# Moving the next head's projection to the second step of a block, and the out-projection to the third

## The chip, the cores and the metric

The kernel runs on one core of one Trainium2 chip. The metric is the time of one execution on the device in microseconds (us). Before the change the median of two runs is 1168.97 us (1168.78 to 1169.16).

## The reference, cut to what matters

The input `x` has 2 batches of 1024 tokens with 128 features. It is layer-normalised to `xn`; the output is `x` plus a differential attention of `xn` plus a mixture-of-experts feed-forward of `xn`. The attention takes nearly all of the time:

```python
Q = einsum('bse,hec->bhsc', X, Wq) + bq      # 16 heads, 2*64 columns
K = einsum('bse,hec->bhsc', X, Wk) + bk
V = einsum('bse,hed->bhsd', X, Wv) + bv
A1 = einsum('bhqd,bhkd->bhqk', Q1, K1) * s   # Q1, K1: first 64 columns
A2 = einsum('bhqd,bhkd->bhqk', Q2, K2) * s   # Q2, K2: last 64 columns
P = softmax(A1) - lam * softmax(A2)
O = P @ V
Y = concat_heads(O) @ Wo + bo                # then a layer norm, scaled by 0.2
```

## The kernel before, in words

**Steps, blocks and heads.** The attention is 256 steps: 2 batches x 16 heads x 8 tiles of 128 queries. One step makes one query tile's scores against all 1024 keys, twice (map 0 for A1, map 1 for A2). Eight steps are a head. Four steps are a block (`QB = 4`); `kb` counts blocks and `j` is the step's place in its block. This text calls the places step 0, 1, 2 and 3. The loop body is 16 steps long, written out once before a hardware loop, once in it, and once after it.

**No scheduler.** The order on each engine is the order in which its `step` function issues. The engines meet through semaphores alone. TensorE makes scores (L597), transposes of the mixed probabilities (L617), P times V (L633), the out-projection (L645) and the projection of the next head (L550). ScalarE takes exponentials (L838), copies transposes out of PSUM (L860) and makes the high half of the projected q and k (L801, L805). VectorE takes row maxima (L1044), inverts the sums of the exponentials (`inv_sums`, L1073 and L1074), makes the low half of q and k (`low_part`, L981 and L987), copies P times V out (L1102) and adds the out-projection to `y_acc` (`add_y`, L1056). GpSimd scales and mixes the two maps (L514, L517).

**PSUM.** Six of the eight banks are three slots of two banks, taken in turn by the tiles in the list `TILES`: map 0 and map 1 of each step, and a projection tile after the tiles of the steps in `PROJ_AT`. A tile may be written when the tile three places ahead of it in the list has been read: a score tile by its exponential, a projection tile by `low_part` (`slot_free`, L200). Bank 6 (`pt_ps`) takes the transposes. Bank 7 (`o_ps`) takes P times V and then, once that has been copied to `o_t`, the out-projection; so the next P times V in it waits until `add_y` has read it (`after(pe, y_evac, blk)`, L628).

**One step on TensorE** (L649): the scores of map 0 begin; the second half of the transposes of an earlier tile; the rest of the scores, with a wait for map 1's slot in the middle (L672); the first half of the next transposes; the last scores. Behind that comes what belongs to the place in the block: in step 3 the first half of P times V for the block before, in step 0 the other half, in step 1 the out-projection, and in step 2 the projection of the next head (in one block of the head its q, in the other its k).

**One step on ScalarE** (L863): first the high half of a projection made in the step before, then a copy of transposes, the exponential of map 0, a second copy, the exponential of map 1. The second copy is of transposes that TensorE makes at the start of its *next* step. In a step in `PROJ_AT` the exponential of map 1 is ahead of that second copy (L872, L876).

**One step on VectorE** (L1066): row maximum of map 0, `low_part` in a step behind a projection, row maximum of map 1. The `inv_sums` of the step before waits for both of its exponentials; in step 3 it is issued ahead of the first row maximum, and ahead of both stands `add_y`.

**The other queues.** SyncE (`prepare`, L355) waits for the low half of q, swaps its halves by four DMAs (`cross_q`), loads V and reloads weights. GpSimd splits the weights of a head two ahead at the end of a head (`split_w`, L405).

Of the kernel before, what the change touches and what calls it, by code (L numbers as in the profile page):

```python
# [20 lines left out]
QB = 4  # L21
# [15 lines left out]
V_EARLY = 24  # L37
SQRT_AT = 5
BODY = 2 * TB
PROJ_AT = (2, 6)  # L40
SPLIT_W_AT = 7
W_COLS = 5 * D
NW = 2
# [5 lines left out]
def build(nc, X, Wq, bq, Wk, bk, Wv, bv, Wo, bo, gamma, beta, lam,  # L49
# [5 lines left out]
    with ExitStack() as ctx:  # L55
# [112 lines left out]
        def after(eng, s, count):  # L168

            if not isinstance(count, int) or count > 0:  # L170
                eng.wait_ge(s, count)

        def now(g, k, lag=0):

            return not isinstance(g, int) or 0 <= g * BODY + k - lag < STEPS
# [19 lines left out]
        for k in range(BODY):  # L195
            TILES += [(k, 0), (k, 1)] + [(k, "proj")] * (k % TB in PROJ_AT)
        SLOT = {tile: n % 3 for n, tile in enumerate(TILES)}
        assert len(TILES) % 3 == 0

        def slot_free(g, tile):  # L200
# [5 lines left out]
            if what == "proj":  # L206
                return lo_done, 2 * (2 * g + k // TB) + 3 + PROJ_AT.index(k % TB)
            return exp_done, 2 * (g * BODY + k) + what + 1
# [11 lines left out]
        def v_out(u):  # L220


            count = sum(by_act(w) == by_act(u) for w in range(u + 1))
            return (v_copied if by_act(u) else v_evac), count
# [303 lines left out]
        def _(pe):  # L528
# [56 lines left out]
            def open_scores(g, k, s):  # L585
                free = slot_free(g, (k, s))
                if free:
                    pe.wait_ge(*free)

            def product(g, k, s, t, half):  # L590


                a, ax, b = ((q_hi, qx_hi, k_hi), (q_lo, qx_lo, k_hi), (q_hi, qx_hi, k_lo))[t]
                q0, k0 = k // TB * S + (k % TB) * P, k // TB * S
                r = (s + half) % 2
                rows = slice(r * D, (r + 1) * D)
                return pe.matmul(slot[SLOT[k, s]][:, half * BANK:(half + 1) * BANK],  # L597
                                 (ax if half else a)[rows, q0:q0 + P],
                                 b[rows, k0 + half * BANK:k0 + (half + 1) * BANK], start=t == 0, stop=t == 2)
# [49 lines left out]
            def step(g, k):  # L649
                kb, j = divmod(k, QB)  # L650
                if now(g, k):
                    if k % TB == 0:
                        pe.wait_ge(lo_done, 2 * (g * 2 + k // TB) + 2)
                        pe.wait_ge(q_crossed, 64 * (g * 2 + k // TB + 1))
                    if isinstance(g, int) and (g, k) == (0, 1):
                        pe.wait_ge(*v_out(V_EARLY - 2))
                        pe.wait_ge(*v_out(V_EARLY - 1))
                    open_scores(g, k, 0)
                    product(g, k, 0, 0, 0)

                if now(g, k, LAG + 1):
                    open_turn(g, k - 1, 1)
                    turn(k - 1, 1, 0)
                if now(g, k):
                    product(g, k, 0, 1, 0)
                if now(g, k, LAG + 1):
                    turn(k - 1, 1, KC // 2).then_inc(pt_ready, 1)
                if now(g, k):
                    product(g, k, 0, 2, 0)
                    product(g, k, 0, 0, 1)  # L670
                    product(g, k, 0, 1, 1)
                    open_scores(g, k, 1)  # L672
                    product(g, k, 1, 0, 1)
                    product(g, k, 0, 2, 1).then_inc(s_ready, 1)
                    product(g, k, 1, 1, 1)
                    product(g, k, 1, 0, 0)
                    product(g, k, 1, 2, 1)

                if now(g, k, LAG):
                    open_turn(g, k, 0)  # L680
                    turn(k, 0, 0)
                if now(g, k):
                    product(g, k, 1, 1, 0)
                if now(g, k, LAG):
                    turn(k, 0, KC // 2).then_inc(pt_ready, 1)
                if now(g, k):
                    product(g, k, 1, 2, 0).then_inc(s_ready, 1)
                if isinstance(g, int) and g == 0:
                    for u in V_LATE.get(k, ()):
                        values(u)  # L690
                back = 1 if j == 3 else 2
                if j in (3, 0) and now(g, k - j, back * QB):
                    pv(g, kb - back, 0 if j == 3 else 4)
                    pv(g, kb - back, 2 if j == 3 else 6)
                if j == 1 and now(g, k - j, 2 * QB):
                    out_proj(g, kb)
                if k % TB in PROJ_AT and now(g, k, -TB):
                    free = slot_free(g, (k, "proj"))
                    if free:
                        pe.wait_ge(*free)  # L700
                    proj(g * 2 + k // TB + 1, (k // TB + 1) % 2, 32 * (g + k // TB + 1), PROJ_AT.index(k % TB), slot[SLOT[k, "proj"]])

# [53 lines left out]
        def _(act):  # L756
# [106 lines left out]
            def step(g, k):  # L863
                p = k - 1
                if p % TB in PROJ_AT and now(g, p, -TB):
                    high_part(g * 2 + p // TB + 1, (p // TB + 1) % 2, PROJ_AT.index(p % TB),
                              slot[SLOT[p, "proj"]])
# [43 lines left out]
        def _(dve):  # L911
# [129 lines left out]
            def row_max(g, k, s):  # L1041
                m = (k % 2) * 2 + s
                dve.wait_ge(s_ready, 2 * (g * BODY + k) + s + 1)
                dve.tensor_reduce(neg_max[:, m:m + 1], slot[SLOT[k, s]], AX.X, ALU.max, negate=True)\  # L1044
                    .then_inc(max_done, 1)

            def add_y(g, kb):

                if isinstance(g, int) and g == 0 and kb == 2:
                    dve.wait_ge(y_started, 1)  # L1050
                dve.wait_ge(y_mm, g * (BODY // QB) + kb - 1)
                tile0 = (g * 2 + kb // 2 - 1) // H * TB + (kb % 2) * QB
                for t in range(QB):
                    tile = y_acc[:, bass.ds((tile0 + t) * E, E)]
                    r1 = (((kb - 2) * QB + t) % BODY) * 2
                    add = dve.scalar_tensor_tensor(out=tile, in0=o_ps[:, t * E:(t + 1) * E],  # L1056
                                                   scalar=l_inv[:, r1:r1 + 1], in1=tile,
                                                   op0=ALU.mult, op1=ALU.add)
                add.then_inc(y_evac, 1)
# [6 lines left out]
            def step(g, k):  # L1066
                kb, j = divmod(k, QB)
                m, km = g * BODY + k - 1, (k - 1) % BODY
                l, r, e = (km % 4) * 2, km * 2, km % 4
                def inv_sums():  # L1070
                    dve.wait_ge(exp_done, 2 * m + 2)
                    after(dve, scaled, m - 3)
                    dve.reciprocal(l_inv[:, r:r + 2], l_sum[:, l:l + 2]).then_inc(recip_done, 1)  # L1073
                    dve.tensor_scalar(l1_neg[:, e:e + 1], l_sum[:, l:l + 1], lam_neg, None, ALU.mult)\  # L1074
                        .then_inc(recip_done, 1)

                if j == 3 and now(g, k - j, 2 * QB):
                    add_y(g, kb)
                if j == 3 and now(g, k, 1):
                    inv_sums()  # L1080
                if now(g, k):
                    row_max(g, k, 0)
                soon = isinstance(g, int) and g == 0 and k < TB
                if (j == 1 or soon and j != 3) and now(g, k, 1):
                    inv_sums()
                p = k - 1
                if p % TB in PROJ_AT and now(g, p, -TB):
                    low_part(g * 2 + p // TB + 1, (p // TB + 1) % 2, PROJ_AT.index(p % TB),
                             slot[SLOT[p, "proj"]])
                if now(g, k):  # L1090
                    row_max(g, k, 1)
                if j in (0, 2) and not soon and now(g, k, 1):
                    inv_sums()
                if isinstance(g, int) and g == 0:
                    for u in V_LATE.get(k, ()):
                        evac_v(u, u + 1)
                if isinstance(g, int) and (g * BODY + k - 1) in SPLIT_AT:
                    for s_ in SPLIT_AT[g * BODY + k - 1]:
                        low_w1(s_)
                if j == 0 and now(g, k - j, 2 * QB):  # L1100
                    dve.wait_ge(pv_done, g * (BODY // QB) + kb - 1)
                    dve.tensor_copy(o_t[:, (kb % 2) * BANK:(kb % 2 + 1) * BANK], o_ps).then_inc(o_evac, 1)  # L1102
# [86 lines left out]
```

## Time and profile before

| what | us |
|---|---|
| median of 2 runs | 1168.97 |
| the profiled execution | 1167.64 |
| its span in the profile | 1165.7 |
| TensorE busy | 1121.7 (96%) |
| GpSimd busy | 977.9 (84%) |
| ScalarE busy | 955.4 (82%) |
| VectorE busy | 903.6 (78%) |
| chain that ended last | TensorE 67%, ScalarE 22%, issue 6% |

The chain is the work that ended last, followed back from the end of the program. A busy TensorE is not one at its peak, since the ends of matmuls are modelled. The granted clock of TensorE was 0.999 of full speed over the span.

### The profile page before, as it was taken

The page shows a single profiled execution, that of the slowest core. Times are in us where ns is not written, and L with a number is a line of the kernel's source. Part 1 is how long each engine was busy: PE and PEld are TensorE (multiplying, and loading weights), DVE is VectorE, ACT ScalarE, POOL GpSimd, SP SyncE. Part 2 cuts the span into 40 slices and gives each one's busy share as a digit, 9 for nine tenths or more (in the row PEclk, how much of TensorE's full clock was granted, in tenths as well). Part 3 has the DMA queues.
Part 4 walks back from the last instruction along what each step waited for, and adds up shares of the span by engine and source line. Part 5 has one row for each costly group of instructions (what it writes and reads, how often), then busy time and mean ns, then how long its engine had stood idle before and what let it go on. Part 6 is the DMA issues. An engine that isn't in the chain of part 4 may idle for free.

```text
span 1165.7 us, 27852 instructions
## 1 busy us (share of the span) xinstructions
PE 1121.7 (96%) x9730; PEld 775.1 (66%) x9730; DVE 903.6 (78%) x1572; ACT 955.4 (82%) x1722; POOL 977.9 (84%) x607
## 2 busy tenths in 40 slices
PE   5899999999999999999999999999999999998898
PEld 4666666666666666666666666666666666665697
DVE  7888888888888888888888888888888888875610
ACT  3598889898889988888988888888889888986432
POOL 2799999999999999999998999999898888996000
PEclk9999999999999999999999999999999999999999
DMA  8733522222221122222212211222222122100000
GB/s 202 290 87 83 126 58 50 62 62 62 62 58 38 45 62 57 56 67 56 56 45 56 53 33 38 57 56 56 56 56 57 45 56 55 28 22 1 1 19 19
DMA packets 76440, 71.28 MB, mean 61 GB/s; under 512 B 43381, under 2 KB 65397, under 8 KB 76405
## 3 DMA queue, kind: packets, MB, share of 16 engines
q1 hardware_dynamic: 75396, 70.65, 23.4%
q8 instruction: 19, 0.31, 0.1%
q10 hardware_dynamic: 880, 0.19, 0.1%
q14 instruction: 17, 0.13, 0.0%
q0 software_dynamic: 128, 0.01, 0.0%
HBM read 22.59 MB, written 14.68 MB: 32 GB/s over the span
## 4 chain that ended last, share of the span: by engine, by line
PE 67%; ACT 22%; issue 6%; DVE 3%; DMA 1%; ACTq 1%; SPq 0%; DVEq 0%
PE ps L633 21%; PE ps L597 19%; ACT work L838 12%; PE ps L617 11%; PE ps L550 9%; ACT p_mix L838 6%; PE ps L726 3%; ACT pt L860 3%; PE ps L713 2%; PE ps L568 1%; PE ps L645 1%; ACT small L792 1%; DMA v_scratch<-pt 0%; DVE pt L1001 0%; DVE p_mix L957 0%
## 5 line engine op out<-in xcount | busy, mean ns | idle before, releaser
L1044 DVE TENSOR_REDUCE small<-ps 128x1 f32<-128x1024 f32 x512 | 613.5, 1219 | 159.2 <-PE ps L597 159.2
L517 POOL TENSOR_TENSOR p_mix<-p_mix,work 128x1024 f32<-128x1024 f32 x256 | 608.9, 2378 | 21.4
L860 ACT ACTIVATE pt<-ps 128x512 f32<-128x512 f32 x512 | 306.9, 599 | 122.4 <-PE ps L617 120.4
L617 PE MATMUL ps<-ident,p_mix 64*128 64x64 f32 x4096 | 351.2, 226 | 4.1 <-issue 2.2
L514 POOL TENSOR_SCALAR work<-work,small 128x1024 f32<-128x1024 f32 x256 | 308.2, 1204 | 43.6 <-DVE small L1074 41.1
L617 PEld LDWEIGHTS ps<-ident,p_mix 64*128 64x128 f32 x4096 | 303.9, 139 | 51.9 <-issue 32.7
L838 ACT ACTIVATE p_mix<-ps,small 128x1024 f32<-128x1024 f32 x256 | 286.5, 1119 | 3.9 <-DVE small L1044 3.9
L838 ACT ACTIVATE work<-ps,small 128x1024 f32<-128x1024 f32 x256 | 285.2, 1114 | 0.2
L633 PE MATMUL ps<-pt,v_h 128*64 128x512 f32 x1024 | 248.1, 605 | 0.7 <-ACT pt L860 0.7
L597 PE MATMUL ps<-k_hi,q_hi 64*128 64x512 f32 x512 | 226.6, 443 | 4.1 <-ACT p_mix L838 3.5
L597 PE MATMUL ps<-k_hi,q_lo 64*128 64x512 f32 x512 | 224.7, 439 | 0.0
L597 PE MATMUL ps<-k_lo,q_hi 64*128 64x512 f32 x512 | 206.6, 403 | 0.0
L597 PE MATMUL ps<-k_hi,qx_hi 64*128 64x512 f32 x512 | 196.5, 460 | 1.3 <-ACT p_mix L838 1.3
L597 PEld LDWEIGHTS ps<-k_hi,q_hi 64*128 64x128 f32 x512 | 94.3, 184 | 137.4 <-ACT p_mix L838 70.6
L597 PE MATMUL ps<-k_lo,qx_hi 64*128 64x512 f32 x512 | 172.6, 397 | 0.0
L597 PE MATMUL ps<-k_hi,qx_lo 64*128 64x512 f32 x512 | 170.4, 392 | 0.0
L633 PEld LDWEIGHTS ps<-pt,v_h 128*64 128x64 f32 x1024 | 62.3, 136 | 94.2 <-issue 93.3
L597 PEld LDWEIGHTS ps<-k_hi,q_lo 64*128 64x128 f32 x512 | 94.4, 184 | 0.0
L597 PEld LDWEIGHTS ps<-k_lo,q_hi 64*128 64x128 f32 x512 | 94.0, 184 | 0.2
L597 PEld LDWEIGHTS ps<-k_lo,qx_hi 64*128 64x128 f32 x512 | 91.6, 185 | 3.0
L597 PEld LDWEIGHTS ps<-k_hi,qx_hi 64*128 64x128 f32 x512 | 81.8, 189 | 17.8 <-ACT work L838 8.1
L597 PEld LDWEIGHTS ps<-k_hi,qx_lo 64*128 64x128 f32 x512 | 92.9, 187 | 0.9
(137 smaller groups left out, 1212.8 us busy)
## 6 DMA issues: line engine op xcount, KB each, us to landing
qx_hi<-q_hi SPq DMA_DIRECT2D x64, 256.0 KB, 3.8
qx_lo<-q_lo SPq DMA_DIRECT2D x64, 256.0 KB, 4.7
v_scratch<-pt SPq DMA_DIRECT2D x16, 512.0 KB, 4.8
v_h<-v_scratch SPq DMA_DIRECT2D x32, 256.0 KB, 3.1
w_scratch<-wqk_hi SPq DMA_DIRECT2D x16, 160.0 KB, 1.8
w_scratch<-wqk_lo SPq DMA_DIRECT2D x16, 160.0 KB, 1.9
wqk_hi<-w_scratch SPq DMA_DIRECT2D x16, 160.0 KB, 2.2
wqk_lo<-w_scratch SPq DMA_DIRECT2D x16, 160.0 KB, 2.3
```

The source lines that it names most:

```text
L514: pool.tensor_scalar(e2, e2, l_inv[:, 2 * km + 1:2 * km + 2], l1_neg[:, km % 4:km % 4 + 1], ALU.mult, ALU.mult).then_inc(scaled, 1)
L517: pool.tensor_tensor(e1, e1, e2, ALU.add).then_inc(mix_done, 1)
L550: mm = pe.matmul(into[:, half * BANK:(half + 1) * BANK], wt[:, col:col + P], a[:, bass.ds(t0 + half * BANK, BANK)], start=j == 0, stop=j == 2)
L568: mm = pe.matmul(v_bank(u), a[:, i * P:(i + 1) * P], w[:, hv * BANK:(hv + 1) * BANK], start=j == 0, stop=j == 2)
L597: return pe.matmul(slot[SLOT[k, s]][:, half * BANK:(half + 1) * BANK], (ax if half else a)[rows, q0:q0 + P], b[rows, k0 + half * BANK:k0 + ...
L617: mm = pe.transpose(pt_ps[:, c * D:(c + 1) * D], p_mix[rows, col:col + P], ident[rows, rows])
L633: mm = pe.matmul(o_ps[half * D:(half + 1) * D, :], vh4[:, (kb // 2) % 2, c, :], pt4[:, kb % 2, c, :], start=c < 2, stop=c >= KC - 2, skip_ ...
L713: mm = pe.matmul(slot[u % 3][:, half * BANK:(half + 1) * BANK], w[set_][:, c * P:(c + 1) * P], a[:, t0:t0 + BANK], start=j == 0, stop=j == 2)
L726: mm = pe.matmul(out_ps, hidden[u % 4][:, t * P:(t + 1) * P], w24[:, 0 if f == 0 else TOPK * b + f, c, :], start=i == 0 and t % 4 == 0, st ...
L838: act.activation((p_mix, e2_buf)[s][:, k % 4 * S:(k % 4 + 1) * S], slot[SLOT[k, s]], ACT.Exp, bias=neg_max[:, m:m + 1], scale=1.0, accum_o ...
L860: act.activation(pt4[:, kb % 2, :, j * P + half * D:j * P + (half + 1) * D], pt_ps.rearrange("p (c q) -> p c q", c=KC), ACT.Copy).then_inc ...
L1044: dve.tensor_reduce(neg_max[:, m:m + 1], slot[SLOT[k, s]], AX.X, ALU.max, negate=True)\
```

## The change

Three things move. `PROJ_AT` becomes (1, 5), so the projection of the next head stands behind step 1 of each block and not behind step 2; with it move its place in the list of tiles, the step in which ScalarE and VectorE read it (now step 2, before step 3), and the steps in which ScalarE has the exponential of map 1 ahead of the second copy (now step 1, before step 2). The out-projection goes from step 1 to step 2. `add_y` stays in step 3, and goes from ahead of `inv_sums` to behind the first row maximum. No operation is added or removed.

```diff
-PROJ_AT = (2, 6)
+PROJ_AT = (1, 5)
...
-                if j == 1 and now(g, k - j, 2 * QB):
+                if j == 2 and now(g, k - j, 2 * QB):
                     out_proj(g, kb)
...
-                if j == 3 and now(g, k - j, 2 * QB):
-                    add_y(g, kb)
                 if j == 3 and now(g, k, 1):
                     inv_sums()
                 if now(g, k):
                     row_max(g, k, 0)
+                if j == 3 and now(g, k - j, 2 * QB):
+                    add_y(g, kb)
```

VectorE, steps 1 to 3 of the last block ahead of the loop, before. L1044 is a row maximum, L1073 and L1074 are `inv_sums`, L1056 is `add_y`, L987 is `low_part` of k.

```order
L1044 TENSOR_REDUCE small<-ps 128x1 x3
L1073 RECIPROCAL small<-small 128x2
L1074 TENSOR_SCALAR small<-small 128x1
L1056 SCALAR_TENSOR_TENSOR y_acc<-ps,small,y_acc 128x128 x4
L1073 RECIPROCAL small<-small 128x2
L1074 TENSOR_SCALAR small<-small 128x1
L1044 TENSOR_REDUCE small<-ps 128x1
L987 SCALAR_TENSOR_TENSOR k_lo<-ps,small,k_hi 128x512 x2
L1044 TENSOR_REDUCE small<-ps 128x1
```

The same place now:

```order
L1044 TENSOR_REDUCE small<-ps 128x1 x2
L987 SCALAR_TENSOR_TENSOR k_lo<-ps,small,k_hi 128x512 x2
L1044 TENSOR_REDUCE small<-ps 128x1
L1073 RECIPROCAL small<-small 128x2
L1074 TENSOR_SCALAR small<-small 128x1
L1073 RECIPROCAL small<-small 128x2
L1074 TENSOR_SCALAR small<-small 128x1
L1044 TENSOR_REDUCE small<-ps 128x1
L1056 SCALAR_TENSOR_TENSOR y_acc<-ps,small,y_acc 128x128 x4
L1044 TENSOR_REDUCE small<-ps 128x1
```

`low_part` has gone from step 3 into step 2, and the four additions of `add_y` now stand behind the `inv_sums` of step 2 and behind a row maximum of step 3; before, they stood ahead of both.

ScalarE, steps 2 and 3 of a block in the loop, before. L860 copies transposes, `p_mix` is map 0's exponential, `work` map 1's, L805 the high half of k; in brackets stand the semaphores waited for.

```order
L860 ACTIVATE pt<-ps 128x8x64 [waits pt_ready]
L832 ISA
L838 ACTIVATE p_mix,small<-ps,small 128x1024 [waits pt_ready,max_done]
L832 REGISTER_ALU
L838 ACTIVATE work,small<-ps,small 128x1024 [waits mix_done,max_done]
L860 ACTIVATE pt<-ps 128x8x64 [waits pt_ready]
L797 REGISTER_ALU [waits bias_ready]
L805 ACTIVATE k_hi<-ps,small 128x512 [waits proj_mm]
L805 ACTIVATE k_hi<-ps,small 128x512
```

The same engine now, from the second copy of step 1 to the exponential of map 1 of step 2:

```order
L860 ACTIVATE pt<-ps 128x8x64 [waits pt_ready]
L797 REGISTER_ALU [waits bias_ready]
L805 ACTIVATE k_hi<-ps,small 128x512 [waits proj_mm]
L805 ACTIVATE k_hi<-ps,small 128x512
L860 ACTIVATE pt<-ps 128x8x64 [waits pt_ready]
L832 ISA
L838 ACTIVATE p_mix,small<-ps,small 128x1024 [waits pt_ready,max_done]
L860 ACTIVATE pt<-ps 128x8x64 [waits pt_ready]
L832 REGISTER_ALU
L838 ACTIVATE work,small<-ps,small 128x1024 [waits mix_done,max_done]
```

In step 2 the exponential of map 1 (`work`) stood directly behind that of map 0. Now a copy stands between them, the one that waits for transposes which TensorE makes in step 3.

## Rows read from the trace of the kernel before

**Rows 1.** The page: busy time of each engine and its share.

```profile
PE 1121.7 (96%) x9730; PEld 775.1 (66%) x9730; DVE 903.6 (78%) x1572; ACT 955.4 (82%) x1722; POOL 977.9 (84%) x607
```

**Rows 2.** Waits: engine, line, whom for; us in total, times, longest.

```profile
PEld ps L597 <- ACT p_mix L838: 73.3, 122, 2.0
```

**Rows 3.** Timeline of PE, one block: start, us, engine, line, tiles, count, [idle before].

```profile
504.16 0.49 PE L597 MATMUL ps<-k_hi,q_hi 64*128 64x512 f32 x1
...
508.23 0.50 PE L597 MATMUL ps<-k_hi,q_hi 64*128 64x512 f32 x1
...
510.43 1.16 PE L645 MATMUL ps<-wo_dup,o_t 128*128 x8
511.52 0.49 PE L597 MATMUL ps<-k_hi,q_hi 64*128 64x512 f32 x1
...
514.06 0.73 PE L550 MATMUL ps<-xT_hi,wqk_hi 128*128 x2 [0.16 <-ACT work L838]
...
515.65 0.50 PE L597 MATMUL ps<-k_hi,q_hi 64*128 64x512 f32 x1
...
516.74 0.50 PE L597 MATMUL ps<-k_hi,qx_hi 64*128 64x512 f32 x1
...
518.23 1.94 PE L633 MATMUL ps<-pt,v_h 128*64 128x512 f32 x8
520.09 0.49 PE L597 MATMUL ps<-k_hi,q_hi 64*128 64x512 f32 x1
```

**Rows 4.** Timeline of ACT (ScalarE) in the same block.

```profile
509.03 0.60 ACT L860 ACTIVATE pt<-ps 128x512 f32<-128x512 f32 x1 [0.80 <-PE ps L617]
509.52 1.11 ACT L838 ACTIVATE work<-ps,small 128x1024 f32<-128x1024 f32 x1
...
510.61 0.60 ACT L860 ACTIVATE pt<-ps 128x512 f32<-128x512 f32 x1
...
515.47 1.14 ACT L838 ACTIVATE work<-ps,small 128x1024 f32<-128x1024 f32 x1
516.46 0.23 ACT L838 ACTIVATION_READ_ACCUMULATOR work<-ps,small 128x1 f32 x1
...
517.03 1.30 ACT L805 ACTIVATE k_hi<-ps,small 128x512 fp32r<-128x512 f32 x2
```

**Rows 5.** Timeline of DVE (VectorE) in the same block.

```profile
509.73 1.22 DVE L1044 TENSOR_REDUCE small<-ps 128x1 f32<-128x1024 f32 x1 [0.69 <-PE ps L597]
510.87 0.15 DVE L1073 RECIPROCAL small<-small 128x2 f32<-128x2 f32 x1
...
511.05 1.21 DVE L1044 TENSOR_REDUCE small<-ps 128x1 f32<-128x1024 f32 x1
...
515.48 1.11 DVE L1056 SCALAR_TENSOR_TENSOR y_acc<-ps,small,y_acc 128x128 f32 x4
516.72 0.17 DVE L1073 RECIPROCAL small<-small 128x2 f32<-128x2 f32 x1
...
518.43 1.40 DVE L987 SCALAR_TENSOR_TENSOR k_lo<-ps,small,k_hi 128x512 fp32r<-128x512 f32 x2
```

**Rows 6.** Groups by line: busy us, mean ns of one | idle before.

```profile
L981 DVE SCALAR_TENSOR_TENSOR q_lo<-ps,small,q_hi 128x1024 fp32r<-128x1024 f32 x32 | 40.8, 1274 | 0.0
```

**Rows 7.** Timeline of PE: out-projections of the third block and the last.

```profile
77.96 1.16 PE L645 MATMUL ps<-wo_dup,o_t 128*128 128x128 f32 x8
...
1054.56 1.16 PE L645 MATMUL ps<-wo_dup,o_t 128*128 128x128 f32 x8
```

**Rows 8.** Timeline of PE in the last two blocks, which have no projection.

```profile
1043.84 0.49 PE L597 MATMUL ps<-k_hi,q_hi 64*128 64x512 f32 x1 [1.74 <-ACT p_mix L838]
...
1059.77 0.50 PE L597 MATMUL ps<-k_hi,q_hi 64*128 64x512 f32 x1 [1.73 <-ACT p_mix L838]
...
1063.48 2.06 PE L633 MATMUL ps<-pt,v_h 128*64 128x512 f32 x8
```

**Rows 9.** One stretch: length; busy PE, PEld, DVE, ACT, POOL; granted clock; DMA.

```profile
1060.60:1064.00 3.40, 3.40 (x21) 2.55 (x21) 2.03 (x5) 1.24 (x5) 3.32 (x3) 0.53 0.00 0
```

## The prediction

> **What bounds the kernel now.** I read the page first: TensorE is busy 96% of the span, GpSimd 84%, ScalarE 82% [rows 1]. That share says little here, so I went on to the waits: 73.3 us in which TensorE's weight loads for scores waited for an exponential of map 0 [rows 2]. Then I laid one block out in time on three engines [rows 3 to 5]. TensorE sets the pace in steps 0 and 1: step 0 lasts 508.23 - 504.16 = 4.07 us, of which the second half of P times V is the end, and step 1 lasts 511.52 - 508.23 = 3.29 us, 2.20 of scores and 1.09 of out-projection. Around the projection ScalarE sets it. Step 2 lasts 515.65 - 511.52 = 4.13 us, with a wait ahead of the projection and one behind it, and the scores of step 3 take 518.23 - 515.65 = 2.58 us and not 2.20, because the slot of map 1 came free only at 516.74. A block is 16.01 us: (1054.56 - 77.96) / 61 from the third block's out-projection to the last one's [rows 7].
>
> **The change part by part.** Nothing is added, so all of it is in what now stands behind what. I follow one block, with T1, T2, T3 as the starts of TensorE's steps 1, 2 and 3.
>
> *Steps 1 and 2.* ScalarE copies transposes 0.80 after T1 (509.03 - 508.23), starts the exponential left over from step 0 0.49 later, and the next instruction 1.09 after that (510.61) [rows 3, 4]. A second copy is another 0.49; so map 0's exponential of step 1 starts at T1 + 2.87 and has ended, with the reading of its sum, 1.22 later (515.47 to 516.69 [rows 4]), at T1 + 4.09. In the new list of tiles the first tile of step 2 takes the slot of that one, as the first tile of step 3 did before: T2 = T1 + 4.15. TensorE by itself would be ready at T1 + 2.20 + about 1.35 of projection. Map 1's exponential of step 1 now comes directly behind (its row maximum lands about T1 + 4.03: 511.05 + 1.21 - 508.23 [rows 5]), ends at T1 + 5.3 and frees the slot of the second tile of step 2. From such a release to the end of the scores is 518.23 - 516.74 = 1.49 us [rows 3]: T1 + 6.8. The out-projection adds 1.09: TensorE stands ready for step 3 at T1 + 7.9.
>
> *The slot of step 3.* The first tile of step 3 now takes the projection's slot, three tiles back, so it waits for `low_part`. That stands behind the first row maximum of step 2, which starts 0.55 after the release (517.29 by the same block, 0.29 of idle behind 516.72 and its 0.28) and holds VectorE 1.14: T1 + 7.0. The high half is ready then (copy 0.49, k in 1.30, from T1 + 5.2). The low half of k takes 1.40 [rows 5], of q 1.27 [rows 6]. T3 is T1 + 8.45 or T1 + 8.32, mean **8.4**, where steps 1 and 2 took 3.29 + 4.13 = 7.42 in this block. The projection's own waits are not cured; they come one step earlier, and a short step follows.
>
> *Step 3, the large term.* P times V at its end writes the bank that `add_y` has to read first. Before, `add_y` stood first in step 3 and ran 515.48 to 516.59 [rows 5], while P times V started at 518.23: 1.6 us in hand. Now the chain is: the second copy of step 2 waits for transposes that TensorE makes at the start of step 3 (0.80); then comes the exponential of map 1 (0.49 to its start, 1.22 to its end); `inv_sums` waits for it (0.03 and 0.18, as 516.72 behind 516.69 and 511.05 behind 510.87); the row maximum holds VectorE 1.14 (510.87 - 509.73); the four additions take 1.11; P times V takes up the release in some 0.05. The sum is 5.02, against the 2.20 at which its turn comes. TensorE stands idle for 2.8 us, about 2.65 between the records. Its own 1.86 (520.09 - 518.23) follows: step 3 lasts **6.88**. Moving `add_y` alone would cost less; it is the lost early exponential of step 2, in front of `inv_sums`, that makes the chain this long.
>
> *Step 0* stays at 4.07: the exponential of map 1 waits for TensorE's next transposes as it did before, its row maximum long since done.
>
> The block is 8.4 + 6.88 + 4.07 = 19.35, against 16.01: +3.34. `add_y` stands in 62 blocks of the loop (the third to the last), so **+207 us**. The last two have no projection, but the row [rows 8] shows that they wait for exponentials all the same. The first two have no `add_y`; their steps 1 and 2 may gain 1 us each, and I leave that as part of the bound of 9 us (0.15 per block, for places where a tenth was read off).
>
> *The clock.* Twice in the trace TensorE idled 1.7 us in the midst of attention: 1.74 ahead of 1043.84 and 1.73 ahead of 1059.77 [rows 8]. Behind the first nothing happened. Behind the second the granted clock fell to the lower level, 1.2 GHz, for most of a stretch of 3.40 us (0.53 in it [rows 9]): 3.71 us from the step's start to P times V, where a step with a late slot took 2.58 and one without 2.20. One fall costs 1.1 to 1.5 us by these rows, at most 1.6 (3.40 x 0.47). The idle of 2.65 us in each new block is half as long again as either. Between no fall and one in every block I take three in four, nearest to the row that fell, at 1.4 us: 62 x 0.75 x 1.4 = **+65 us**; both steps behind the idle, P times V and step 0, are at TensorE's pace, so the loss stays. The Trainium skill, "TensorE: Matmul & The Clock Gate", in "A second HAM failure mode: psum-queue depth-cycling", says that a kernel that waits on PSUM between groups of matmuls swings between the two clocks and pays after each burst; the row at 1059.77 agrees, the one at 1043.84 does not, and this rule speaks against the change.
>
> *The other queues.* GpSimd's work is 977.9 us over 256 steps, 3.8 us a step [rows 1], and a longer block hides it with more room; its weight split is needed one step earlier, in blocks that are 3 us longer. SyncE's crossing of q and the reload of weights wait for `low_part` of q and the last projection, both now a step earlier, and have nothing late behind them. Both at nothing; if the blocks did not grow, the split would be the first to be late.
>
> **The sum.** 207 + 65 = 272 us. The profiled execution took 1167.64, the median is 1168.97, 1.3 above it: 1168.97 + 272 = **1441 us**.
>
> **Rivals.**
>
> *The clock stays up.* The step changes are as above, and the new idle does no more than the one ahead of 1043.84. Time: 1168.97 + 207 = 1376. For it: one of two gaps left the clock alone, and the page shows full clock nearly throughout. Against: the new gap is longer, and comes 62 times. The same page of the Trainium skill, in "The HAM clock gate", has the fall come behind a window that is idle. Read as no work in it at all, that gives this rival's time, since matmuls run on both sides of the gap; the row at 1059.77 contradicts such a reading. Chance 0.25.
>
> *The exponential comes in time.* If ScalarE had map 1 of step 2 finished before step 3, `add_y` would wait for the row maximum only: 1.50 (509.73 - 508.23) + 1.14 + 1.11 + 0.05 = 3.80, so 1.6 of idle and a block of 18.15. 62 x 2.14 = +133: 1302, or up to 1345 with some falls of the clock. Against it stands the order of ScalarE: the copy ahead of that exponential needs transposes of step 3. Chance 0.06.
>
> *Not slower.* P times V would have to find its bank free, that is `add_y` ended before T3 + 2.2, and `low_part` before TensorE wants its slot. Then the waits around the projection could vanish too, since ScalarE idles 0.80 at the start of step 1 [rows 4] and would meet the projection less late. A block would be TensorE's own work, 3.55 + 3.29 + 4.07 + 4.07 = 14.98: 62 x -1.03 = -64, 1105 us. It decides at 2.2 us behind T3; the chain above gives 5.02, and its shortest form 3.80. A wait read wrongly in the code is what is left for it. Chance 0.02; half of that with only the waits cured in part, near no change, is counted apart as 0.02.
>
> *More.* The clock falls in every block and the half-speed stretch makes the next exponentials late too: above 1485. Chance 0.05.
>
> **How the numbers follow.** The forecast has 0.60. Its own range is 1168.97 + 207 - 9 + 62 x 0.5 x 1.1 = 1401 to 1168.97 + 207 + 9 + 62 x 1.6 = 1484. The rival with the full clock, 1376 less 9 and a little for the tenths, has to be in the range, so it is 1360 to 1480; the rival of 1302 and those of the other sign lie outside it. A measurement of this kernel tells 2% from no change. Slower by more than that is 0.60 + 0.25 + 0.06 + 0.05 = 0.96, within 2% 0.02, faster 0.02.
>
> **What would show it.** In the changed profile: P times V of L633 with an idle of about 2.6 us ahead of it, put down to VectorE's L1056, 62 times, some 165 us; step 3 of about 6.9 us and step 0 unchanged where the clock is whole; scores of step 3 that wait for `low_part` by half a microsecond; `inv_sums` in step 3 held by L838; stretches at a granted clock under 1 all through attention, behind the idle. Wrong would be: L1056 ending before the scores of step 3 do; a block of 16 us; a clock of 1.00 throughout, which takes the 65 us away; or a fall in every block, which makes it 90 to 100.

## The result, and the profile after

The changed kernel takes 1491.77 us (1488.93 and 1494.61 in two runs) against 1168.97 us, a ratio of 1.276 (95% interval 1.273 to 1.279). The forecast was 1441 us and its range ended at 1480, so the direction and the mechanism in the main were right and the size was missed by 51 us, 12 of them beyond the range. The profiled execution took 1488.93 us with a span of 1487.0 us, 321.3 us more than that of before.

The page after, busy time of each engine and the granted clock in 40 slices; the first row answers to [rows 1]:

```profile
PE 1228.4 (83%) x9730; PEld 803.3 (54%) x9730; DVE 898.1 (60%) x1572; ACT 965.5 (65%) x1722; POOL 974.6 (66%) x607
PEclk9998989998989898999998989998989999899999
```

The instructions are as many as before and VectorE, ScalarE and GpSimd are as long busy; TensorE is 107 us longer busy with the same matmuls, and the clock row shows an 8 in 11 of its 40 slices where the row of before had nines alone.

The waits after (engine, line, for whom; us in total, times, longest); the row of `p_mix` answers to [rows 2]:

```profile
PE ps L633 <- DVE y_acc L1056: 129.2, 45, 2.9
...
DVE small L1073 <- ACT work L838: 89.1, 64, 3.3
PEld ps L597 <- ACT p_mix L838: 78.1, 127, 2.1
...
PE ps L633 <- issue: 47.6, 17, 2.8
```

P times V waits for the additions, `inv_sums` for the exponential of map 1, once per block; the wait for map 0's exponentials, from which the prediction started, is hardly changed. The 129.2 us are 45 waits of 2.87; 17 more of 2.8 us stand in the last row, under "issue" and not under their releaser.

Now one block in which the clock did not fall, TensorE first, from one out-projection to the next. It answers to [rows 3].

```profile
298.12 1.16 PE L645 MATMUL ps<-wo_dup,o_t 128*128 x8
...
299.69 0.50 PE L597 MATMUL ps<-k_hi,q_hi 64*128 64x512 f32 x1 [0.41 <-DVE q_lo L981]
...
304.92 1.94 PE L633 MATMUL ps<-pt,v_h 128*64 128x512 f32 x8 [2.84 <-DVE y_acc L1056]
306.79 0.49 PE L597 MATMUL ps<-k_hi,q_hi 64*128 64x512 f32 x1
...
310.85 0.50 PE L597 MATMUL ps<-k_hi,q_hi 64*128 64x512 f32 x1
...
313.39 0.72 PE L550 MATMUL ps<-xT_hi,wqk_hi 128*128 x2 [0.28 <-ACT work L838]
...
317.66 1.16 PE L645 MATMUL ps<-wo_dup,o_t 128*128 x8
```

The block lasts 19.54 us. Step 3 starts at 299.69 behind a wait for the low half of q, and lasts 7.10; step 0 lasts 4.06; steps 1 and 2 take the remaining 8.38.

The chain in that step 3 on ScalarE, and then on VectorE; they answer to [rows 4] and [rows 5].

```profile
300.61 0.60 ACT L860 ACTIVATE pt<-ps 128x512 f32<-128x512 f32 x1 [0.78 <-PE ps L617]
301.10 1.11 ACT L838 ACTIVATE work<-ps,small 128x1024 f32<-128x1024 f32 x1
302.09 0.20 ACT L838 ACTIVATION_READ_ACCUMULATOR work<-ps,small 128x1 f32 x1
```

```profile
302.33 0.17 DVE L1073 RECIPROCAL small<-small 128x2 f32<-128x2 f32 x1 [1.38 <-ACT work L838]
302.41 0.19 DVE L1074 TENSOR_SCALAR small<-small 128x1 f32<-128x1 f32 x1
302.52 1.21 DVE L1044 TENSOR_REDUCE small<-ps 128x1 f32<-128x1024 f32 x1
303.65 1.12 DVE L1056 SCALAR_TENSOR_TENSOR y_acc<-ps,small,y_acc 128x128 f32 x4
```

Copy of the transposes, exponential, `inv_sums`, row maximum, additions: each starts as the one before ends, and P times V follows at 304.92, 5.23 us behind the start of the step.

The next excerpt is a block in which the clock fell, on TensorE, and behind it three stretches of the same block (length; busy PE, PEld, DVE, ACT, POOL; granted clock; DMA). The last answers to [rows 9].

```profile
511.27 1.16 PE L645 MATMUL ps<-wo_dup,o_t 128*128 x8
...
512.81 0.49 PE L597 MATMUL ps<-k_hi,q_hi 64*128 64x512 f32 x1 [0.38 <-DVE q_lo L981]
...
517.94 2.87 PE L633 MATMUL ps<-pt,v_h 128*64 128x512 f32 x8 [2.84 <-DVE y_acc L1056]
520.74 0.79 PE L597 MATMUL ps<-k_hi,q_hi 64*128 64x512 f32 x1
...
523.58 1.94 PE L633 MATMUL ps<-pt,v_h 128*64 128x512 f32 x8
...
525.45 0.49 PE L597 MATMUL ps<-k_hi,q_hi 64*128 64x512 f32 x1
```

```profile
517.00:520.50 3.50, 2.56 (x8) 0.70 (x8) 1.92 (x5) 0.99 (x2) 3.42 (x3) 0.76 0.31 74
520.50:524.00 3.50, 3.50 (x32) 2.61 (x32) 1.13 (x1) 1.98 (x4) 0.92 (x1) 0.75 0.00 0
524.00:528.00 4.00, 3.73 (x37) 2.13 (x33) 3.15 (x6) 3.09 (x7) 2.40 (x2) 1.00 0.29 66
```

The idle is the same 2.84. Behind it P times V takes 520.74 - 517.94 = 2.80 us to the next step, where it took 1.87 at full clock, and the scores of step 0 take 2.84, where they took 2.2. The two first stretches have granted clocks of 0.76 and 0.75, so the clock was at its lower level for about half of each.

**Where the 321 us went.** From the first out-projection in the loop to the last one, 61 blocks, the mean block is 21.18 us (85.02 to 1377.17), against 16.01 [rows 7]. In the record of the granted clock 57 stretches at the lower level lie in these blocks, 12 of them twice as long as the others, 235.5 us in all. Five of the 61 blocks have none, and last 19.58 on average; the 43 with one stretch of the usual length last 21.05, the 12 with one of double length 22.30. So the new order costs 3.57 us a block, 62 x 3.57 = 221 us, and the clock another 1.60, 62 x 1.60 = 99 us. Together 320 of the 321. Of the 57 stretches 55 come next behind the wait for the additions; the other two come behind waits of 1.85 us for map 0's exponential, one in each of the last two blocks, which have no projection [rows 8].

### The profile page after: what moved, and what is told of

Same layout as the page of the kernel before. It is cut to its first block, busy times and chain, and to the rows that moved or that the text cites. A ratio compares the mean times of both kernels' runs of the same rounds, so it can differ in the third digit from the quotient of the medians.

```text
span 1487.0 us, 27838 instructions
## 1 busy us (share of the span) xinstructions
PE 1228.4 (83%) x9730; PEld 803.3 (54%) x9730; DVE 898.1 (60%) x1572; ACT 965.5 (65%) x1722; POOL 974.6 (66%) x607
## 4 chain that ended last, share of the span: by engine, by line
PE 58%; issue 15%; DVE 12%; ACT 12%; DVEq 1%; DMA 1%; ACTq 1%; SPq 0%
PE ps L633 22%; PE ps L597 15%; ACT work L838 10%; PE ps L617 9%; PE ps L550 7%; DVE y_acc L1056 3%; DVE q_lo L981 3%; PE ps L726 2%; DVE k_lo L987 2%; PE ps L713 2%; DVE small L1044 2%; ACT pt L860 1%; DVE small L1074 1%; DVEq L1056 0%; PE ps L568 0%
## 5 line engine op out<-in xcount | busy, mean ns | idle before, releaser
L1044 DVE TENSOR_REDUCE small<-ps 128x1 f32<-128x1024 f32 x512 | 617.9, 1217 | 407.2 <-PE ps L597 407.0
L860 ACT ACTIVATE pt<-ps 128x512 f32<-128x512 f32 x512 | 305.4, 596 | 367.6 <-PE ps L617 366.1
L633 PE MATMUL ps<-pt,v_h 128*64 128x512 f32 x1024 | 329.6, 776 | 177.5 <-DVE y_acc L1056 129.2
L617 PE MATMUL ps<-ident,p_mix 64*128 64x64 f32 x4096 | 361.7, 230 | 3.2 <-issue 2.2
L617 PEld LDWEIGHTS ps<-ident,p_mix 64*128 64x128 f32 x4096 | 310.2, 143 | 51.5 <-issue 39.8
L838 ACT ACTIVATE p_mix<-ps,small 128x1024 f32<-128x1024 f32 x256 | 286.0, 1117 | 66.7 <-DVE small L1044 66.7
L838 ACT ACTIVATE work<-ps,small 128x1024 f32<-128x1024 f32 x256 | 284.4, 1111 | 1.5 <-DVE small L1044 1.3
L597 PE MATMUL ps<-k_hi,q_hi 64*128 64x512 f32 x512 | 234.6, 458 | 32.6 <-DVE k_lo L987 16.9
L633 PEld LDWEIGHTS ps<-pt,v_h 128*64 128x64 f32 x1024 | 80.4, 163 | 299.6 <-issue 298.7
L597 PEld LDWEIGHTS ps<-k_hi,q_hi 64*128 64x128 f32 x512 | 98.7, 193 | 208.4 <-issue 91.1
L597 PE MATMUL ps<-k_lo,qx_hi 64*128 64x512 f32 x512 | 165.6, 406 | 0.0
L597 PE MATMUL ps<-k_hi,qx_lo 64*128 64x512 f32 x512 | 163.5, 401 | 0.0
L1073 DVE RECIPROCAL small<-small 128x2 f32<-128x2 f32 x256 | 40.2, 157 | 89.2 <-ACT work L838 89.1
```

The lines of the kernel that those rows point to most:

```text
L617: mm = pe.transpose(pt_ps[:, c * D:(c + 1) * D], p_mix[rows, col:col + P], ident[rows, rows])
L633: mm = pe.matmul(o_ps[half * D:(half + 1) * D, :], vh4[:, (kb // 2) % 2, c, :], pt4[:, kb % 2, c, :], start=c < 2, stop=c >= KC - 2, skip_ ...
L838: act.activation((p_mix, e2_buf)[s][:, k % 4 * S:(k % 4 + 1) * S], slot[SLOT[k, s]], ACT.Exp, bias=neg_max[:, m:m + 1], scale=1.0, accum_o ...
L860: act.activation(pt4[:, kb % 2, :, j * P + half * D:j * P + (half + 1) * D], pt_ps.rearrange("p (c q) -> p c q", c=KC), ACT.Copy).then_inc ...
```

## The experiments

Each run was compared with the kernel before on the same chip. "Block" is the mean from the first to the last out-projection in the loop, "free" the mean of the blocks that no stretch at the lower clock touches, "falls" the number of such stretches in those 61 blocks, "idle" the longest wait or two that TensorE shows in a block of that run. Block, free, falls and idle are those of the one execution whose trace was kept.

| kernel | us | ratio (95%) | block | free | falls | idle in a block |
|---|---|---|---|---|---|---|
| before | 1169 | 1 | 16.01 | 16.01 | 0 | small |
| changed | 1491.8 | 1.276 (1.273 to 1.279) | 21.18 | 19.58 | 57 | 2.84 |
| e1, filler | 1391.4 | 1.189 (1.187 to 1.192) | 19.55 | 19.53 | 2 | 0.28 and 0.46 |
| e2, additions first | 1231.9 | 1.054 (1.051 to 1.056) | 17.02 | 17.02 | 0 | 0.15 |
| e3, additions late only | 1266.2 | 1.083 (1.077 to 1.089) | 17.51 | 17.47 | 1 | 1.44 |
| e4, `inv_sums` behind | 1329.9 | 1.137 (1.131 to 1.143) | 18.54 | 18.36 | 7 | 1.69 |
| e5, early exponential | 1446.9 | 1.238 (1.235 to 1.242) | 20.51 | 19.31 | 43 | 1.05 and 1.26 |
| e9, that and the maximum | 1402.5 | 1.200 (1.197 to 1.204) | 19.77 | 19.49 | 16 | 1.52 and 1.69 |
| e6, projection only | 1274.7 | 1.091 (1.088 to 1.094) | 17.69 | 17.31 | 21 | 1.71 |
| e7, out-projection only | 1192.9 | 1.021 (1.018 to 1.024) | 16.44 | 16.44 | 0 | small |
| e8, short filler | 1446.1 | 1.236 (1.231 to 1.241) | 20.46 | 19.54 | 36 | 0.28 and 1.56 |

Two things have to be kept in mind with the falls. First, the last two blocks have no projection and wait 1.7 to 1.9 us for map 0's exponential in most of these kernels; behind that wait, and not behind the one that the run is about, stand both falls of e1, the one of e3, one each of e4 and e5 and two each of e8 and e9. Second, executions of one kernel differ. The other run of e3 had a mean clock of 0.988 and took 1271.1 us where the one with the trace had 0.996 and 1261.2; for e4 they are 0.980 and 1334.9 against 0.989 and 1324.8. So those two kernels have more falls in one execution than the table counts. In the changed kernel and in e5, e6, e8 and e9 the clocks of the two runs lie within 0.005 of each other.

### The clock apart from the idle (e1)

```diff
+                if j == 3 and now(g, k - j, 2 * QB) and now(g, k, -1):
+                    g1, k1 = (g, k + 1) if k + 1 < BODY else (g + 1, 0)
+                    pe.wait_ge(*slot_free(g1, (k1, 0)))
+                    for _ in range(8):
+                        pe.matmul(slot[SLOT[k1, 0]][:, 0:BANK], xT_hi[:, 0:P], xT_hi[:, 0:BANK], start=True, stop=True)
                 back = 1 if j == 3 else 2
```

> The changed kernel, with eight matmuls without use (128x128 by 128x512, into the slot that the next step will overwrite) put on TensorE where it waits for the additions of add_y, 62 times. They need about 1.7 us at full clock and fit into the 2.8 us of wait. Theory A (the idle itself costs 3.57 us a block, and the clock that it brings down another 1.60): the granted clock is 1.00 throughout attention, a block lasts 19.6 us as the five blocks without a fall do, and the time is 1169 + 62 x 3.6 = 1390 us. Rival B (the clock is low for another reason, such as the shorter share of TensorE's work in a block, or its fall costs nothing that the idle does not cost anyway): clock about 0.92 and a time of 1480 us or more, since the filler only adds work.

Measured: 1391.4 us, a mean clock of 0.992, two falls in the 61 blocks. One block of it on TensorE, L695 being the matmuls without use, and below it the wait ahead of the first of the two falls:

```profile
476.61 1.16 PE L645 MATMUL ps<-wo_dup,o_t 128*128 x8
...
478.15 0.50 PE L597 MATMUL ps<-k_hi,q_hi 64*128 64x512 f32 x1 [0.38 <-DVE q_lo L986]
...
480.71 2.11 PE L695 MATMUL ps<-xT_hi 128*128 128x512 f32 x8 [0.28 <-ACT work L843]
...
483.29 1.94 PE L633 MATMUL ps<-pt,v_h 128*64 128x512 f32 x8 [0.46 <-DVE y_acc L1061]
...
1254.90 0.67 PE L597 MATMUL ps<-k_hi,q_hi 64*128 64x512 f32 x1 [1.86 <-ACT p_mix L843]
```

P times V still starts 5.14 us behind the start of step 3, since the additions release it no earlier; the block is as long as a block of the changed kernel whose clock stayed up. More work made the kernel 100 us faster. That settles the split: about 221 us are the new order, about 100 the clock. It is the idle ahead of P times V that brings the clock down: with work in it no fall comes behind it in the 61 blocks, where 55 did, and the two that are left come behind the wait of the last two blocks. Rival B's price, a fall that costs nothing of its own, is out; its other half, the share of TensorE's work in a block, is not, since the filler raises that too. e9 below settles it.

### The place of the additions (e2, e3, e4)

In e2 `add_y` goes back to its old place in the changed kernel:

```diff
+                if j == 3 and now(g, k - j, 2 * QB):
+                    add_y(g, kb)
                 if j == 3 and now(g, k, 1):
                     inv_sums()
                 if now(g, k):
                     row_max(g, k, 0)
-                if j == 3 and now(g, k - j, 2 * QB):
-                    add_y(g, kb)
```

> The changed kernel with add_y back ahead of inv_sums in step 3; projection and out-projection stay at their new places. Theory A (add_y behind inv_sums and a row maximum is the large term): P times V waits a tenth of a microsecond at most, step 3 is about 4.3 us, the block about 17.1 us (the slot chain of steps 1 and 2 alone adds 1.1), and the clock stays at 1.00: 1169 + 62 x 1.1 = 1237 us. Rival C (the new place of the projection is what costs, through the slot that low_part frees late): the block stays above 19 us and the time above 1350.

Measured: 1231.9 us, block 17.02, no fall. In its step 3 on TensorE the wait is 0.15 us, where the expectation had a tenth at most:

```profile
428.07 0.50 PE L597 MATMUL ps<-k_hi,q_hi 64*128 64x512 f32 x1 [0.38 <-DVE q_lo L981]
...
430.51 1.94 PE L633 MATMUL ps<-pt,v_h 128*64 128x512 f32 x8 [0.15 <-DVE y_acc L1056]
432.37 0.50 PE L597 MATMUL ps<-k_hi,q_hi 64*128 64x512 f32 x1
```

Step 3 lasts 4.30 and not 7.10. Of the 323 us, 260 hang on where four short additions stand. Rival C fell.

e3 is the reverse: the kernel before with that one edit, `add_y` behind `inv_sums` and the row maximum.

> The kernel before with nothing changed but add_y behind inv_sums and the first row maximum of step 3. There the exponential of map 1 of step 2 is early, so the additions end 1.64 + 1.14 + 1.11 = 3.9 us after the start of step 3 and P times V waits 1.35 us instead of none. Theory A: 1169 + 62 x 1.35 = 1253 us, with few or no falls of the clock, since the idle is shorter than the 1.7 us that once brought it down. Rival C (the place of add_y matters little): under 1190. Rival D (any idle of a microsecond in each block brings the clock down): 1169 + 62 x 2.7 = 1340.

Measured: 1266.2 us, block 17.51 (17.47 free), one fall; P times V waits 1.44 us for the additions. The fall comes behind another wait, in the last block but one:

```profile
1131.95 0.50 PE L597 MATMUL ps<-k_hi,q_hi 64*128 64x512 f32 x1 [1.74 <-ACT p_mix L838]
```

Theory A was 13 us low; rival C was wrong, and so was rival D: in the execution with the trace no fall comes behind 1.44 us of idle. The other run, 10 us slower at the lower mean clock, had more falls; behind which waits no trace shows, so an idle of this length is not cleared. The same move that costs 1.50 a block here costs 4.16 in the changed kernel (21.18 against 17.02): 2.56 without any fall, since the chain ahead of the additions is longer there, and 1.60 by the clock.

e4 is the changed kernel with the order row maximum, additions, `inv_sums`:

```diff
-                if j == 3 and now(g, k, 1):
-                    inv_sums()
                 if now(g, k):
                     row_max(g, k, 0)
                 if j == 3 and now(g, k - j, 2 * QB):
                     add_y(g, kb)
+                if j == 3 and now(g, k, 1):
+                    inv_sums()
```

> The changed kernel with inv_sums of step 3 behind add_y: row maximum, additions, inv_sums. It takes the wait for the late exponential out of the way to the additions. Theory A: step 3 is 1.5 + 1.14 + 1.11 + 0.05 + 1.87 = 5.7 us instead of 7.1, the idle 1.6 us instead of 2.8, the block 18.3 us without falls: 1169 + 62 x 2.3 = 1311 us with the clock at 1.00, up to 1375 if it still falls in most blocks (an idle of 1.7 did so once out of twice). Rival C (the projection's new place costs, not this wait): above 1450.

Measured: 1329.9 us, free block 18.36 (18.3 expected), seven falls, six of them behind the wait for the additions. Rival C was wrong. One step 3 of it:

```profile
456.21 0.49 PE L597 MATMUL ps<-k_hi,q_hi 64*128 64x512 f32 x1 [0.38 <-DVE q_lo L981]
460.19 1.94 PE L633 MATMUL ps<-pt,v_h 128*64 128x512 f32 x8 [1.69 <-DVE y_acc L1056]
```

So the wait of `inv_sums` for the late exponential is 1.2 us of the chain, and since without it the idle is 1.69 and not 2.84, it is worth 50 falls as well: 162 us in all.

### Why the exponential is late (e5, e9)

The prediction said that the chain is long because the early exponential of step 2 was lost. e5 gives it back:

```diff
+EARLY = (1, 2, 5, 6)
...
-                if k % TB in PROJ_AT and now(g, k):
+                if k % TB in EARLY and now(g, k):
                     exps(g, k, 1)
...
-                if k % TB not in PROJ_AT and now(g, k):
+                if k % TB not in EARLY and now(g, k):
```

> The changed kernel with the exponential of map 1 ahead of the second copy in step 2 as well as in step 1, as the kernel before had it in step 2. The prediction said that the loss of this early exponential is what makes the chain to the additions long. By that sentence step 3 falls from 7.1 to 5.7 us, a block without falls to 18.2 and the time to about 1311 us or somewhat more. Rival E (low_part now stands ahead of the row maximum of map 1 in step 2, so that the exponential cannot start before about 1.2 us behind the start of step 3, whatever its place): step 3 stays at 6.8 to 7.1, the idle at 2.6 to 2.8, the falls stay, and the time is 1470 to 1495 us.

Measured: 1446.9 us, free block 19.31. ScalarE and VectorE of e5 around the start of step 3 at 520.60 (an inserted line puts L838 at L839, L987 at L988, and so on):

```profile
519.45 1.11 ACT L839 ACTIVATE p_mix<-ps,small 128x1024 f32<-128x1024 f32 x1
520.45 0.20 ACT L839 ACTIVATION_READ_ACCUMULATOR p_mix<-ps,small 128x1 f32 x1
521.71 1.12 ACT L839 ACTIVATE work<-ps,small 128x1024 f32<-128x1024 f32 x1 [1.06 <-DVE small L1045]
```

```profile
519.15 1.40 DVE L988 SCALAR_TENSOR_TENSOR k_lo<-ps,small,k_hi 128x512 fp32r<-128x512 f32 x2
520.47 1.21 DVE L1045 TENSOR_REDUCE small<-ps 128x1 f32<-128x1024 f32 x1
```

ScalarE is free for the exponential at 520.65 and waits 1.06 us for its row maximum, which stands on VectorE behind `low_part`. The sentence of the prediction was wrong: the exponential would be late by its maximum even if it came first. The early exponential gives 0.27 us a block, not 1.2. Rival E had that right, with its time 23 us too high, since there were 43 falls and not 57. One step 3 of e5 on TensorE shows what may be the reason:

```profile
704.42 0.50 PE L598 MATMUL ps<-k_hi,q_hi 64*128 64x512 f32 x1 [0.39 <-DVE q_lo L982]
...
707.32 0.24 PE L618 MATMUL ps<-ident,p_mix 64*128 64x64 f32 x1 [1.05 <-issue]
...
709.35 3.60 PE L634 MATMUL ps<-pt,v_h 128*64 128x512 f32 x8 [1.26 <-DVE y_acc L1057]
```

The transposes of this step (L618) and its last scores, which now stand behind the late copy, lie in the middle of the gap and part it in two. That this is what spares some of the falls was not tried by itself; e8, which puts work into the gap, points the same way.

e9 adds the other half, the row maximum of map 1 ahead of `low_part`:

```diff
+                if now(g, k):
+                    row_max(g, k, 1)
                 if p % TB in PROJ_AT and now(g, p, -TB):
                     low_part(...)
-                if now(g, k):
-                    row_max(g, k, 1)
```

> As the run with the early exponential in step 2, and in addition VectorE takes the row maximum of map 1 of step 2 ahead of low_part. Rival E: now the exponential ends before step 3 and step 3 falls to 5.7 us, but low_part frees the slot of step 3 later by the 1.14 us of the maximum, so a block without falls is again about 19.4 us; its idle is in two pieces of 1.6 us each, so the clock falls in few blocks: 1169 + 62 x 3.4 = 1380, at most 1420 us. The prediction's sentence (the early exponential alone is worth 1.2 us a block): 1311 us.

Measured: 1402.5 us, free block 19.49, 16 falls. On TensorE:

```profile
523.18 0.50 PE L598 MATMUL ps<-k_hi,q_hi 64*128 64x512 f32 x1 [1.52 <-DVE q_lo L982]
...
527.24 1.94 PE L634 MATMUL ps<-pt,v_h 128*64 128x512 f32 x8 [1.69 <-DVE y_acc L1057]
```

The idle before P times V shrinks to 1.69 and the one before step 3 grows from 0.4 to 1.52. The free block is as long as ever; the microsecond went from one wait into the other, and all that was gained is 41 falls. The time is inside the expectation's 1380 to 1420 us. This answers what e1 left open: TensorE has the same work here as in the changed kernel, in a block as long (19.49 against 19.58 free), and 16 falls instead of 57. So it is not the share of TensorE's work in a block that decides, but how the idle lies in it; here 2.4 us of work stand between the two pieces.

### The two moves apart (e6, e7)

e6 is the kernel before with `PROJ_AT = (1, 5)` alone, e7 the kernel before with the out-projection at `j == 2` alone.

> The kernel before with the projection at the second step and nothing else: the out-projection stays behind it in the same step 1, and add_y first in step 3. Theory A, in which the projection's place costs by the slot that low_part frees: step 1 is 1.09 longer, step 2 has scores alone, and TensorE then waits some 1.7 us for low_part at step 3. The block is about 17.4 us and the time 1169 + 62 x 1.4 = 1256 us, with few falls. Rival F (the place of the projection is free as long as the additions come in time, and the 1.0 us a block of the run with add_y first came from the out-projection's move): under 1190 us.

Measured: 1274.7 us, free block 17.31, 21 falls. The first scores of step 3 wait 1.71 us for the low half:

```profile
441.33 0.50 PE L597 MATMUL ps<-k_hi,q_hi 64*128 64x512 f32 x1 [1.71 <-DVE q_lo L981]
```

> The kernel before with the out-projection behind step 2, ahead of the projection, and nothing else. Theory A: the out-projection leaves step 1 without its 1.09 us of cover, the copies and exponentials come late by some of it, and in step 2 the projection starts 1.09 later, which meets its slot long free; the block is about 16.3 us and the time 1169 + 62 x 0.3 = 1188 us, clock 1.00. Rival F: 16.9 to 17.0 us a block, 1225 us or more.

Measured: 1192.9 us, block 16.44, no fall. Theory A holds in both and rival F in neither; e6 is 19 us above its expectation, because an idle of 1.71 brought the clock down 21 times where I had put few. Moved together (e2) they cost 1.01 a block, less than the projection alone with its 1.30 without falls: the 1.09 us of out-projection fill most of the wait for `low_part`, which is 1.71 in e6 and 0.38 in e2.

### How much idle (e8)

> The changed kernel with three of the matmuls without use instead of eight, about 0.65 us of work, put ahead of the wait for the additions; some 1.9 us of idle is left behind them, a little more than the 1.7 that brought the clock down once out of twice in the kernel before. Theory A (the clock falls by how long TensorE idles in one piece or nearly so): the falls become fewer than the 57 of the changed kernel but do not vanish, 5 to 40 of them; the block without a fall stays at 19.6 us and the time lies between 1395 and 1450 us. Rival G (it falls in any block with over a microsecond of idle): 1480 to 1495 us. Rival H (a pair of matmuls in the gap is enough): 1390 us, clock 0.99.

Measured: 1446.1 us, free block 19.54, 36 falls. A block of it; L695 is the short filler:

```profile
517.64 0.96 PE L695 MATMUL ps<-xT_hi 128*128 128x512 f32 x3 [0.28 <-ACT work L843]
520.16 1.94 PE L633 MATMUL ps<-pt,v_h 128*64 128x512 f32 x8 [1.56 <-issue]
```

That is what theory A expected, and rivals G and H fell. Between the fillers of none, three and eight matmuls the falls behind the wait for the additions go 55, 34, 0, at the same free block.

## Why the prediction was wrong, point by point

**What bounds the kernel.** ScalarE's exponentials set the pace around the projection, TensorE elsewhere: so the rows of before show it, and nothing in the runs speaks against it.

**Steps 1 and 2.** Predicted 8.4 us, measured 8.38 in the block shown. The wait for `low_part` at step 3, with half a microsecond, is there: 0.41 for q in the block shown, 0.51 for k in the block before it.

**Step 3.** Predicted 6.88, measured 7.10. The chain is as told, link by link; it has 5.23 us in that block and not 5.02. Two links carry the difference: the copy starts 0.92 behind the step (299.69 to 300.61) where I put 0.80, and the release of P times V by the additions takes 1.27 from their start (303.65 to 304.92) where I put 1.16. What was told about its cause was wrong in part: the exponential is late by two things at once, its place on ScalarE and its maximum's place on VectorE. e5 shows that the second alone makes it late; that the first alone would follows from the order on ScalarE and was not run.

**Step 0.** Predicted 4.07, measured 4.06 at full clock.

**The sum of the order.** Predicted 3.34 a block and 207 us, measured 3.57 and 221. The bound of 9 us was too small by 5: it allowed for tenths in the blocks and not for a link that is systematically longer.

**The clock. This is the step that failed**, in the amount of it: "Between no fall and one in every block I take three in four", each at one length. There were 57 falls in the 61 blocks, 12 of them twice as long, which makes 69 lengths where three in four of 62 makes 46.5. The price was right: 99 us over 69 is 1.43 each, against 1.4. So 65 us became 99. Of the 34 us between them about 15 are the share (57 falls and not 46.5), about 17 the twelve falls of double length, for which the sum had no term, and 2 the price. With the 14 us of the order that makes 48 of the 51. By the same reckoning the kernel would have taken some 1475 us had no fall been double, inside the range; that it lay outside hangs on something that nothing in the trace of before could show. The share could have been put higher: the idle was half as long again as one that had brought the clock down. The two gaps of 1.7 us [rows 8] were a fair guide to gaps of 1.7 us (6 falls behind them in e4, 21 in e6, 14 in e9 with two such gaps), not to one of 2.84. The forecast's own upper end had a fall in every block, at 1.6, 99 us; but the published range stopped at 1480.

**The rival called More.** It had a fall in every block and a time above 1485, with a chance of 0.05, and it is the one that came, near enough. That the low clock makes the next exponentials late too, its other half, is not needed for 1.43 us a fall, and no run tries it.

**The page on the clock.** The Trainium skill, "TensorE: Matmul & The Clock Gate", "A second HAM failure mode: psum-queue depth-cycling", has a kernel that idles between groups of matmuls swing between the clocks and pay for it between the bursts. The changed kernel does so, 57 times, and e1 shows the pay: 100 us. The first rival read the same page's section "The HAM clock gate" so that matmuls on both sides of each gap keep the clock up. The trace refutes that reading: in the changed kernel 55 falls come behind gaps with matmuls on both sides.

**The other rivals.** The clock that stays up: 1376 was told. It did not come, but e1, which holds the clock up by filling the gap, took 1391, that time with the 14 us of the order. The exponential in time: 1302 was told, and e4, which takes the same wait out of the chain, measured 1330. Not slower: nothing of it; what it needs, the additions ahead, gave 1232 in e2.

**The other queues.** At nothing, as told: GpSimd's busy time is 974.6 against 977.9 [rows 1], and no wait for the split of weights or for SyncE is among the long ones.

## What to carry to other kernels

Where one PSUM bank serves two uses in turn, the read that frees it belongs ahead of everything on its engine that waits for this step's work: four additions of 1.1 us in all, moved behind one wait and one maximum, cost 4.2 us a block. Where two things make a link late, mending one of them gives little (0.27 us a block in e5), and mending both can move the wait elsewhere (e9), so follow the chain through both engines before naming its cause. And where a change opens a repeated gap on TensorE, price the gap and the clock behind it apart: here the clock was 31% of the loss, and eight useless matmuls in the gap gave it back.

## What the runs showed of the hardware

- A longer single gap on TensorE is followed by a fall of its clock more often: behind gaps of 1.44 us none in the traced execution of e3 (its other run had a lower mean clock, 0.988 against 0.996), 6 and 21 behind gaps of 1.7 (e4, e6), 55 behind gaps of 2.84. Gaps of one length did not act alike in e4 and e6; what makes the difference was not tried.
- A short piece of work inside a gap does not mend it: with 0.96 us of matmuls and 1.56 of idle behind them the clock still fell behind 34 of the gaps (e8), and with gaps of 1.05 and 1.26 us around 0.8 us of work it fell in 43 stretches (e5); with 2.4 us of work between two gaps of 1.52 and 1.69 there were 16 (e9). With eight matmuls in the gap and 0.46 us of idle behind them there were none behind it (e1).
- A fall cost 1.4 us where TensorE had work through it: 21.05 against 19.58 us for a block of the changed kernel. Twelve of its 57 falls lasted twice as long as the others, and what decides that stays open.
